# Value products in quarters over four steps, and positional tiles moved in halves of even and odd partitions

## The chip, the cores and the metric

The kernel runs on one core of one Trainium2 chip. The metric is the device time of one execution in microseconds; for the kernel before it is 3494.53 us, the median of 3 runs (3494.47 to 3496.61).

## What is computed

A Macaron layer over `x` of shape (8, 1024, 256), all in float32: half a feed-forward step, attention with relative positions, half a feed-forward step. What matters here is the attention (16 heads of 16 features, S = 1024):

```python
q = (xn @ Wq + bq).reshape(B, S, H, dh)      # k and v likewise
p = (pe @ Wp).reshape(S, H, dh)
content = jnp.einsum('bihd,bjhd->bhij', q + u_bias, k)
pos = jnp.einsum('bihd,jhd->bhij', q + v_bias, p)
pos = _relative_shift(pos)
attn = jax.nn.softmax((content + pos) * scale, axis=-1)
head = jnp.einsum('bhij,bjhd->bihd', attn, v).reshape(B, S, Dm)

def _relative_shift(pos_score):
    B, Hh, S1, S2 = pos_score.shape
    padded = jnp.concatenate([jnp.zeros((B, Hh, S1, 1), pos_score.dtype), pos_score], axis=-1)
    padded = padded.reshape(B, Hh, S2 + 1, S1)
    return padded[:, :, 1:].reshape(B, Hh, S1, S2)
```

The relative shift is a change of row pitch: rows written 1025 elements apart and read back 1024 apart come out shifted.

## The kernel before, in words

The program has three phases, one after the other: a front phase (first feed-forward step, layer norm, projections), the attention phase, and a closing phase (output projection, second feed-forward step). The change is in the attention phase alone.

The attention phase works on 128 units (batch times head) of 8 tiles each, so 1024 tiles. A tile is 128 query rows by 1024 keys, 512 KB in float32. Each engine runs the same numbered steps, 16 to a pass of its loop (`BODY = 16`, `rounds()`, L612 to L621); the first pass and the last, which is longer to drain what is under way, are written out, and the passes between are a hardware loop. In step `t`

- TensorE (`step`, L755) makes the content scores of tile `t` (`strips` into `ps_con`, L705) and the positional scores of tile `t + LEAD`, `LEAD = 8` (`strips` into `ps_pos`, L705). Both use 32 rows of the array each and run side by side. Then, in two steps of four, come the value products of the last complete group of four tiles (`times_values`, 32 matmuls in each of its two halves, L741), in another step one transpose that turns the heads back (`turn_heads`, L752), and in every step eight transposes of the finished scores of tile `t - 2` (`turn`, L729).
- ScalarE copies the positional scores of tile `t + 8` from PSUM to `pos_out`, a ring of 8 (`copy_positional`, L786), and takes the exponentials of tile `t - 2` (L795).
- SyncE, named SP in the profile, issues every DMA of the phase. It waits until `pos_out` of tile `t + 8` is copied and writes it to DRAM with pitch 1025 (`write`, L651); it then reads back, with pitch 1024, tile `t + 4` into `pos_in`, also a ring of 8 (`read_back`, L663), for which the write of tile `t + 5` must have landed. Steps 0, 1 and 2 of each unit also load queries (L633), keys (L640) and values (L646) of the next unit, and step 7 stores the heads of the last one (L669).
- VectorE adds content and positional scores and takes the row minimum of their negative (`total`, L818); before that it needs the read-back of tile `t` to have landed. In one step of four it copies the value products (L826), in the next it normalises the heads (L832, L837).
- GpSimd subtracts the maximum (L855).

There is one `ps_con`, so TensorE can start the content scores of tile `t + 1` only when VectorE has read those of tile `t` (`content_room`, L709). DRAM row `u` of block `g` of a tile (four blocks of 32 rows) lies in partition `4u + g`. `at_once` (L43) is a wait in an instruction of its own; on SP it blocks everything behind it, and so does each DMA while SP issues it.

Of the kernel before, what the change touches and what calls it, by code (L numbers as in the profile page):

```python
# [9 lines left out]
P = 128  # L10
B, S, D, H = 8, 1024, 256, 16
# [8 lines left out]
GAPS = 4  # L20
HALF = S // 2

TILES = S // P
UNITS = H * B
NT = UNITS * TILES
BODY = 2 * TILES
LEAD = 8
READ_LAG = 4
RING = 8
PITCH = S + 1  # L30
QUAD = 4
# [11 lines left out]
def at_once(eng, sem, value):  # L43

    eng.wait_ge(sem, value)
    eng.nop(nofuse=True)
# [491 lines left out]
def attention_phase(nc, keep, a):  # L538


    with ExitStack() as ctx:
        def sb(name, shape, dt=F32):
            return ctx.enter_context(nc.sbuf_tensor("at_" + name, shape, dt))
# [9 lines left out]

        pos_out = sb("pos_out", [P, RING, S])
        pos_in = sb("pos_in", [P, RING, S])
        neg_max = sb("neg_max", [P, RING])
        prob = [sb(f"prob{k}", [P, TILES, QUAD * P]) for k in range(2)]
# [9 lines left out]

        written, read = sems("written", RING), sems("read", RING)
        q_in, k_in, vals_in, head_out = (sems(n, 2) for n in ("q_in", "k_in", "vals_in", "head_out"))
# [6 lines left out]
        class Tile:  # L576
# [11 lines left out]

            def rounds(self, n, add=0):

                return self.r * (16 * BODY // n) + 16 * (self.t // n + add)

            def units(self, each=1, add=0):
                return self.r * (2 * each) + (self.unit_in_body * each + add)
# [17 lines left out]
        def rounds(eng, step):  # L612

            last = NT // BODY - 1
            for t in range(BODY):
                step(0, t)
            with eng.Fori(1, last) as r:
                for t in range(BODY):
                    step(r, t)
            for t in range(BODY + 10):  # L620
                step(last, t)  # L621

        score_dram = a["scores"]
# [2 lines left out]
        @block.sync  # L626
        def _(sp):
            def load_queries(u):
                if u.past(BODY):
                    at_once(sp, con_mm, u.units(TILES, -TILES))  # L630
                at_once(sp, pos_mm, u.units(TILES))
                rows = 2 * STRIP if u.last_unit() else P
                sp.dma_start(left[u.side][0:rows:2, :],  # L633
                             a["queries"][u.unit() + 1].rearrange("s d m -> (s d) m")[0:rows // 2, :])\
                    .then_inc(q_in[u.side], 16)

            def load_keys(u):
                if u.past(BODY):
                    at_once(sp, con_mm, u.units(TILES, -TILES))
                sp.dma_start(right[u.side][0:2 * STRIP:2, :], a["keys"][u.unit()].rearrange("n d m -> (n d) m"))\  # L640
                    .then_inc(k_in[u.side], 16)

            def load_values(u):
                if u.past(BODY):
                    at_once(sp, v_ready, u.units(1, -1))
                sp.dma_start(v_in[u.side][:, :], a["values"][u.unit(), :, :]).then_inc(vals_in[u.side], 16)  # L646

            def write(w):
                at_once(sp, pos_copied, w.count(1, 1))
                dst = score_dram[w.side, w.i * P * PITCH:(w.i + 1) * P * PITCH]  # L650
                sp.dma_start(dst.rearrange("(g u c) -> u g c", g=GAPS, c=PITCH)[:, :, 1:], pos_out[:, w.slot, :])\  # L651
                    .then_inc(written[w.slot], 16)

            def read_back(t):
                if t.i == 0:
                    at_once(sp, written[t.slot], t.rounds(RING, 1))
                if t.i + 1 < TILES:
                    n = Tile(t.r, t.t + 1)
                    at_once(sp, written[n.slot], n.rounds(RING, 1))
                if t.past(RING):  # L660
                    at_once(sp, turned, t.count(2, 2 - 2 * RING))
                src = score_dram[t.side, (t.i * P + 1) * S:(t.i * P + 1 + P) * S]
                sp.dma_start(pos_in[:, t.slot, :], src.rearrange("(g u c) -> u g c", g=GAPS, c=S))\  # L663
                    .then_inc(read[t.slot], 16)

            def store_head(t):

                at_once(sp, normed, t.units(2, 2))
                sp.dma_start(a["heads"][t.unit(), :, :].rearrange("(g u) n -> u g n", g=GAPS), head[t.side][:, :])\  # L669
                    .then_inc(head_out[t.side], 16)  # L670

            def step(r, t):
                w = Tile(r, t + LEAD)
                if w.real():
                    write(w)
                back = Tile(r, t + LEAD - READ_LAG)
                if back.real():
                    read_back(back)
                for at, load in ((0, load_queries), (1, load_keys), (2, load_values)):
                    if t % TILES == at and Tile(r, t - at + TILES).real():  # L680
                        load(Tile(r, t - at + TILES))
                done = Tile(r, t - TILES)
                if t % TILES == 7 and done.real():
                    store_head(done)

            sp.wait_ge(blanked, 1)
            sp.dma_start(left[1][2 * STRIP:P:2, :], a["queries"][0].rearrange("s d m -> (s d) m")[STRIP:2 * STRIP, :])\
                .then_inc(first_in, 16)
            load_queries(Tile(0, 0))
            load_keys(Tile(0, 0))  # L690
            load_values(Tile(0, 0))
            for w in range(LEAD):
                write(Tile(0, w))
                if w >= READ_LAG:
                    read_back(Tile(0, w - READ_LAG))
            rounds(sp, step)
            for k in range(2):
                sp.wait_ge(head_out[k], 16 * UNITS // 2)

        @block.tensor  # L700
        def _(pe):
# [28 lines left out]
                                           pos_in[:, t.slot, kt * P:(kt + 1) * P], keep["ident"][:, :])  # L730
                    ins.then_inc(turned, 1)

            def times_values(t, half):
                if half == 0:
                    pe.wait_ge(v_ready, t.units(1, 1))
                    pe.wait_ge(exped, t.count(2, 2 * QUAD))
                    if t.past(QUAD):
                        pe.wait_ge(pv_copied, t.quads())
                for kt in range(TILES // 2 * half, TILES // 2 * (half + 1)):
                    for g in range(QUAD):  # L740
                        ins = pe.matmul(ps_pv[VW * g:VW * (g + 1), :], v_aug[t.side][:, kt, :],  # L741
                                        prob[t.t // QUAD % 2][:, kt, g * P:(g + 1) * P],
                                        start=(kt == 0), stop=(kt == TILES - 1))
                if half == 1:
                    ins.then_inc(pv_mm, 1)

            def turn_heads(t):

                pe.wait_ge(pv_copied, t.quads(1))
                if t.past(QUAD):  # L750
                    pe.wait_ge(normed, t.quads())
                pe.transpose(ps_head[:, :, :].rearrange("p g v -> p (g v)"), head_T[:, :], keep["ident"][:, :])\  # L752
                    .then_inc(head_mm, 1)

            def step(r, t):  # L755
                if Tile(r, t).real():
                    content_room(Tile(r, t))
                if Tile(r, t + LEAD).real():
                    positional_room(Tile(r, t + LEAD))
                if Tile(r, t).real():  # L760
                    strips(Tile(r, t), Tile(r, t).side, 0, ps_con, con_mm)
                if Tile(r, t + LEAD).real():
                    strips(Tile(r, t + LEAD), Tile(r, t).side, 2 * STRIP, ps_pos, pos_mm)
                if t % QUAD == 2 and Tile(r, t - 6).real():
                    times_values(Tile(r, t - 6), 0)
                if t % QUAD == 3 and Tile(r, t - 7).real():
                    times_values(Tile(r, t - 7), 1)
                if t % QUAD == 1 and Tile(r, t - 9).real():
                    turn_heads(Tile(r, t - 9))
                if Tile(r, t - 2).real():  # L770
                    turn(Tile(r, t - 2))

# [37 lines left out]
        def _(dve):  # L810
# [11 lines left out]
            def copy_products(t):  # L822
                dve.wait_ge(pv_mm, t.quads(1))
                if t.past(QUAD):
                    dve.wait_ge(head_mm, t.quads())
                dve.tensor_copy(head_T[:, :], ps_pv[:, :]).then_inc(pv_copied, 1)  # L826
# [12 lines left out]
                                  ALU.mult).then_inc(normed, 1)  # L839

            def step(r, t):
                if Tile(r, t).real():
                    total(Tile(r, t))
                if t % QUAD == 0 and Tile(r, t - 8).real():
                    copy_products(Tile(r, t - 8))
                if t % QUAD == 1 and Tile(r, t - 9).real():
                    normalise(Tile(r, t - 9))

            rounds(dve, step)

# [284 lines left out]
```

## Time and profile before

| | |
|---|---|
| time, median of 3 runs | 3494.53 us |
| the profiled execution, its own time | 3496.67 us |
| its span | 3494.9 us |
| TensorE busy, share of the span | 3161.2 us, 90% |
| VectorE / ScalarE / GpSimd busy | 1711.3 / 2285.4 / 1330.7 us |
| DMA queue q1, share of 16 engines' span | 95.8% |
| attention, from the first to the last L818 | 337.3 to 3320.0 us |

The page gives each engine's busy time, then the span in 40 slices of 87 us: the attention phase fills slices 4 to 37. Issue instructions of DMAs are not counted as busy on SP; they are found in the timeline (as SPq) and by their source line.

### The profile page before, as it was taken

Reading aid. Unit: us, or ns where it says so; the run is one execution under the profiler, and the core shown is the slowest. Engines: PE = TensorE matmul, PEld = TensorE weight load, DVE = VectorE, ACT = ScalarE, POOL = GpSimd, SP = SyncE. Lnnn points to the kernel's source line nnn. Section 1 sums busy time; section 2 is a strip of 40 time slices with the busy share of each in tenths; the row PEclk is TensorE's granted clock in tenths of the full one; section 3 lists DMA queues with packets and bytes.
Section 4 is the critical chain, followed back from the end, with each engine's and each line's share of the span. In section 5 each row is a group of like instructions: output and inputs, shape, how many; then the busy total and the mean of one; then the engine's idle time right before and its main releaser. Section 6 shows DMA issues by size and latency. Waiting matters only on the chain. (4 is left out here: it accounts for less than half of the span.)

```text
span 3494.9 us, 104304 instructions
## 1 busy us (share of the span) xinstructions
PE 3161.2 (90%) x34876; PEld 1962.1 (56%) x34876; DVE 1711.3 (49%) x3603; ACT 2285.4 (65%) x3255; POOL 1330.7 (38%) x1341
## 2 busy tenths in 40 slices
PE   8996999999999999999999999999999999999988
PEld 5662555555555555555555555555555555555577
DVE  7771444444444444444444444444444444444457
ACT  3443777777767776777777777777777777777633
POOL 2111444444444444444444444444444444444410
PEclk9996999999999999999999999999999999999999
DMA  5977999999999999999999999999999999999862
GB/s 162 296 248 246 376 380 377 379 382 380 378 376 383 379 378 379 383 380 377 378 382 377 380 377 383 381 379 378 381 379 377 379 382 378 380 375 384 332 193 98
DMA packets 433552, 1231.26 MB, mean 352 GB/s; under 512 B 48992, under 2 KB 133472, under 8 KB 433504
## 3 DMA queue, kind: packets, MB, share of 16 engines
q1 hardware_dynamic: 430000, 1229.12, 95.8%
q10 hardware_dynamic: 3504, 1.53, 0.2%
q8 instruction: 27, 0.44, 0.1%
q14 instruction: 21, 0.17, 0.0%
HBM read 617.04 MB, written 613.43 MB: 352 GB/s over the span
## 5 line engine op out<-in xcount | busy, mean ns | idle before, releaser
L818 DVE CUSTOM_DVE_ANT_0 at_pos_in<-at_ps_con,at_pos_in 128x1024 f32<-128x1024 f32 x1024 | 1254.2, 1225 | 1621.7 <-PE at_ps_con L705 1184.4
L855 POOL TENSOR_SCALAR at_pos_in<-at_pos_in,at_neg_max 128x1024 f32<-128x1024 f32 x1024 | 1149.4, 1122 | 1720.3 <-DVE at_neg_max L818 1720.3
L786 ACT ACTIVATE at_pos_out<-at_ps_pos 128x1024 f32<-128x1024 f32 x1024 | 1050.0, 1025 | 651.7 <-PE at_ps_pos L705 651.7
L705 PE MATMUL at_ps_con<-at_right,at_left 32*128 32x512 f32 x4096 | 1157.3, 641 | 262.7 <-DVE at_neg_max L818 261.4
L795 ACT ACTIVATE at_prob<-at_ps_turn 128x512 f32<-128x512 f32 x2048 | 1109.1, 596 | 277.5 <-PE at_ps_turn L729 277.4
L705 PE MATMUL at_ps_pos<-at_right,at_left 32*128 32x512 f32 x4096 | 1164.9, 645 | 28.5 <-DMA at_left<-scratch_queries 20.6
L729 PE MATMUL at_ps_turn<-keep_ident,at_pos_in 128*128 128x128 f32 x8192 | 1105.3, 278 | 0.6 <-ACT at_prob L795 0.6
L729 PEld LDWEIGHTS at_ps_turn<-keep_ident,at_pos_in 128*128 128x128 f32 x8192 | 889.7, 141 | 299.0 <-ACT at_prob L795 188.1
L741 PEld LDWEIGHTS at_ps_pv<-at_prob,at_v_aug 128*32 128x32 f32 x16384 | 416.1, 109 | 387.8 <-issue 246.7
L705 PEld LDWEIGHTS at_ps_con<-at_right,at_left 32*128 32x128 f32 x4096 | 309.5, 183 | 471.7 <-ACT at_pos_out L786 367.6
L741 PE MATMUL at_ps_pv<-at_prob,at_v_aug 128*32 128x128 f32 x16384 | 553.2, 276 | 0.8 <-issue 0.8
L705 PEld LDWEIGHTS at_ps_pos<-at_right,at_left 32*128 32x128 f32 x4096 | 308.6, 184 | 39.9 <-POOL at_v_aug L893 21.0
L752 PEld LDWEIGHTS at_ps_head<-keep_ident,at_head_T 128*128 128x128 f32 x256 | 35.3, 138 | 193.3 <-issue 192.7
L872 POOL COPY at_right<-keep_pos_keys 64x512 f32 (+1 forms) x128 | 78.0, 610 | 37.3 <-POOL at_pos_in L855 20.4
L818 DVE DVE_READ_ACCUMULATOR2_ANT at_neg_max<- 128x1 f32 x1024 | 85.1, 83 | 0.0
L752 PE MATMUL at_ps_head<-keep_ident,at_head_T 128*128 128x128 f32 x256 | 83.8, 328 | 0.4 <-DVE at_head_T L826 0.4
L382 ACT ACTIVATE fr_qk<-fr_ps_qk,keep_b_qk 128x512 f32<-128x512 f32 x64 | 64.4, 1177 | 24.9 <-PE fr_ps_qk L332 24.9
L826 DVE COPY at_head_T<-at_ps_pv 128x128 f32<-128x128 f32 x256 | 73.4, 287 | 3.6 <-PE at_ps_pv L741 3.6
L534 POOL TENSOR_TENSOR fr_scale<-fr_variance,keep_minus_half 128x4 f32<-128x4 f32 x16 | 30.6, 1912 | 116.1 <-DVE fr_variance L456 116.1
L374 ACT ACTIVATE fr_z1T<-fr_ps_a 128x1024 f32<-128x1024 f32 x16 | 16.4, 1026 | 84.1 <-PE fr_ps_a L80 84.1
L1069 POOL TENSOR_TENSOR cl_scale<-cl_variance,keep_minus_half 128x4 f32<-128x4 f32 x16 | 16.1, 1009 | 134.9 <-DVE cl_variance L1051 134.9
L837 DVE TENSOR_TENSOR at_head<-at_ps_head,at_inverse 128x64 f32<-128x64 f32 x256 | 57.6, 225 | 14.3
(90 smaller groups left out, 1296.2 us busy)
## 6 DMA issues: line engine op xcount, KB each, us to landing
scratch_scores<-at_pos_out SPq DMA_DIRECT2D x1024, 512.0 KB, 6.5
at_pos_in<-scratch_scores SPq DMA_DIRECT2D x1024, 512.0 KB, 6.8
scratch_queries<-fr_qk SPq DMA_DIRECT2D x128, 256.0 KB, 4.0
at_left<-scratch_queries SPq DMA_DIRECT2D x127, 256.0 KB, 6.3
fr_x<-in_L_attn_x_dram SPq DMA_DIRECT2D x16, 512.0 KB, 6.0
scratch_x<-fr_x_bo SPq DMA_DIRECT2D x16, 512.0 KB, 5.0
scratch_keys<-fr_qk SPq DMA_DIRECT2D x32, 256.0 KB, 5.0
scratch_values<-fr_values SPq DMA_DIRECT2D x8, 1024.0 KB, 5.8
```

The source lines that it names most:

```text
L382: ins = act.activation(qk[k][:, o, f, :].rearrange("p (t u g) -> p t g u", u=P // GAPS, g=GAPS), ps_qk[:, f, :].rearrange("p (t g u) -> p ...
L705: ins = pe.matmul(banks[:, n, :], left[side][rows, t.i * P:(t.i + 1) * P], right[side][rows, :], start=True, stop=True)
L729: ins = pe.transpose(ps_turn[:, n, j * P:(j + 1) * P], pos_in[:, t.slot, kt * P:(kt + 1) * P], keep["ident"][:, :])
L741: ins = pe.matmul(ps_pv[VW * g:VW * (g + 1), :], v_aug[t.side][:, kt, :], prob[t.t // QUAD % 2][:, kt, g * P:(g + 1) * P], start=(kt == 0) ...
L752: pe.transpose(ps_head[:, :, :].rearrange("p g v -> p (g v)"), head_T[:, :], keep["ident"][:, :])\
L786: act.activation(pos_out[:, t.slot, :], ps_pos[:, :, :].rearrange("p a m -> p (a m)"), ACT.Copy)\
L795: act.activation(prob[t.t // QUAD % 2][:, 4 * n:4 * n + 4, k * P:(k + 1) * P], ps_turn[:, n, :].rearrange("p (j i) -> p j i", i=P), ACT.Exp)\
L818: dve.tensor_tensor_reduce(pos_in[:, t.slot, :], ps_con[:, :, :].rearrange("p a m -> p (a m)"), pos_in[:, t.slot, :], -SCALE, 3.0e38, ALU. ...
L826: dve.tensor_copy(head_T[:, :], ps_pv[:, :]).then_inc(pv_copied, 1)
L837: dve.tensor_tensor(head[t.side][:, :].rearrange("p (t d) -> p t d", d=DH)[:, QUAD * q:QUAD * (q + 1), :], ps_head[:, :, 0:DH], inverse[:, ...
L855: pool.tensor_scalar(pos_in[:, t.slot, :], pos_in[:, t.slot, :], -1.0, neg_max[:, t.slot:t.slot + 1], ALU.mult, ALU.add).then_inc(shifted, 1)
L872: pool.tensor_copy(right[1 - u.side][P // 2:P, :], keep["pos_keys"][P // 2:P, bass.ds(u.unit() % H * HALF, HALF)]).then_inc(p_ready, 1)
```

## The change

The value products of a group of four tiles, so far 32 matmuls in each of two steps, come as 16 in each of four steps; the transpose of the heads, the copy and the normalisation on VectorE move one or two steps later, and on VectorE they stand ahead of the step's `total` instead of behind it. The last pass has 12 further steps instead of 10.

Every positional tile is written as two DMAs of 64 partitions (even ones, then odd ones) and read back the same way. SP's step now reads: wait for the copy, wait for the landed write, write the even half of tile `t + 8`, read the even half of tile `t + 4`, write the odd half, read the odd half. Each DMA is 256 KB. The wait for `turned` ahead of a read is kept only where no write precedes it. A ring slot's semaphore now counts 32 a tile.

```diff
@@ BODY, counts @@
+PARTS = 2
...
-                return self.r * (16 * BODY // n) + 16 * (self.t // n + add)
+                return self.r * (16 * PARTS * BODY // n) + 16 * PARTS * (self.t // n + add)
...
-            for t in range(BODY + 10):
+            for t in range(BODY + 12):
@@ SyncE @@
-            def write(w):
+            def part(rows, n):
+                return rows[:, n:GAPS:PARTS]
+
+            def may_write(w):
                 at_once(sp, pos_copied, w.count(1, 1))
+
+            def write(w, n):
                 dst = score_dram[w.side, w.i * P * PITCH:(w.i + 1) * P * PITCH]
-                sp.dma_start(dst.rearrange("(g u c) -> u g c", g=GAPS, c=PITCH)[:, :, 1:], pos_out[:, w.slot, :])\
+                sp.dma_start(part(dst.rearrange("(g u c) -> u g c", g=GAPS, c=PITCH)[:, :, 1:], n),
+                             pos_out[n:P:PARTS, w.slot, :])\
                     .then_inc(written[w.slot], 16)
...
-                if t.past(RING):
-                    at_once(sp, turned, t.count(2, 2 - 2 * RING))
+
+            def read_back(t, n):
                 src = score_dram[t.side, (t.i * P + 1) * S:(t.i * P + 1 + P) * S]
-                sp.dma_start(pos_in[:, t.slot, :], src.rearrange("(g u c) -> u g c", g=GAPS, c=S))\
+                sp.dma_start(pos_in[n:P:PARTS, t.slot, :],
+                             part(src.rearrange("(g u c) -> u g c", g=GAPS, c=S), n))\
                     .then_inc(read[t.slot], 16)
+
+            def write_and_read(w, back):
+                if w.real():
+                    may_write(w)
+                elif back.real():
+                    at_once(sp, turned, back.count(2, 2 - 2 * RING))
+                if back.real():
+                    may_read(back)
+                for n in range(PARTS):
+                    if w.real():
+                        write(w, n)
+                    if back.real():
+                        read_back(back, n)
@@ TensorE @@
-                if t % QUAD == 2 and Tile(r, t - 6).real():
-                    times_values(Tile(r, t - 6), 0)
-                if t % QUAD == 3 and Tile(r, t - 7).real():
-                    times_values(Tile(r, t - 7), 1)
-                if t % QUAD == 1 and Tile(r, t - 9).real():
-                    turn_heads(Tile(r, t - 9))
+                part = (t - 6) % QUAD
+                if Tile(r, t - 6 - part).real():
+                    times_values(Tile(r, t - 6 - part), part)
+                if part == 0 and Tile(r, t - 10).real():
+                    turn_heads(Tile(r, t - 10))
@@ VectorE @@
+                if t % QUAD == 2 and Tile(r, t - 10).real():
+                    copy_products(Tile(r, t - 10))
+                if t % QUAD == 3 and Tile(r, t - 11).real():
+                    normalise(Tile(r, t - 11))
                 if Tile(r, t).real():
                     total(Tile(r, t))
-                if t % QUAD == 0 and Tile(r, t - 8).real():
-                    copy_products(Tile(r, t - 8))
-                if t % QUAD == 1 and Tile(r, t - 9).real():
-                    normalise(Tile(r, t - 9))
```

On SP, in the loop, the step that also loads the next unit's values and the step behind it stood like this before (names are DRAM and SBUF tensors, the numbers are the DMA's shape):

```order
L651 DMA scratch_scores<-at_pos_out 32x4x1024 [waits at_pos_copied]
L45 REGISTER_ALU [waits at_written7]
L663 DMA at_pos_in<-scratch_scores 128x1x1024 [waits at_turned]
L646 DMA at_v_in<-scratch_values 128x128 [waits at_v_ready]
L45 REGISTER_ALU
L651 DMA scratch_scores<-at_pos_out 32x4x1024 [waits at_pos_copied]
L663 DMA at_pos_in<-scratch_scores 128x1x1024 [waits at_turned]
```

and stand like this now:

```order
L657 DMA scratch_scores<-at_pos_out 32x2x1024 [waits at_pos_copied,at_written7]
L670 DMA at_pos_in<-scratch_scores 64x1x1024
L657 DMA scratch_scores<-at_pos_out 32x2x1024
L670 DMA at_pos_in<-scratch_scores 64x1x1024
L647 DMA at_v_in<-scratch_values 128x128 [waits at_v_ready]
L46 REGISTER_ALU
L657 DMA scratch_scores<-at_pos_out 32x2x1024 [waits at_pos_copied]
L670 DMA at_pos_in<-scratch_scores 64x1x1024
L657 DMA scratch_scores<-at_pos_out 32x2x1024
L670 DMA at_pos_in<-scratch_scores 64x1x1024
```

Two issues a step have become four, back to back; the wait for `turned` is gone, and the wait for the landed write now stands ahead of the write of the same step.

On TensorE, one step of the loop with value products, before:

```order
L705 MATMUL at_ps_pos<-at_right,at_left 128x512 x2
L741 MATMUL at_ps_pv<-at_prob,at_v_aug 32x128 x16
L726 REGISTER_ALU [waits at_shifted]
L729 MATMUL at_ps_turn<-keep_ident,at_pos_in 128x128 [waits at_exped]
L729 MATMUL at_ps_turn<-keep_ident,at_pos_in 128x128 x3
```

and now:

```order
L719 MATMUL at_ps_pos<-at_right,at_left 128x512 x2
L756 MATMUL at_ps_pv<-at_prob,at_v_aug 32x128 x8
L740 REGISTER_ALU [waits at_shifted]
L743 MATMUL at_ps_turn<-keep_ident,at_pos_in 128x128 [waits at_exped]
L743 MATMUL at_ps_turn<-keep_ident,at_pos_in 128x128 x3
```

The row of value products (16 instructions here, 32 matmuls in the trace) is half as long and stands in each of four steps instead of two.

## Rows read from the trace of the kernel before

**Rows 1.** The page, the span in 40 slices: TensorE, its clock, DMA share, rate.
```profile
PE   8996999999999999999999999999999999999988
...
PEclk9996999999999999999999999999999999999999
DMA  5977999999999999999999999999999999999862
GB/s 162 296 248 246 376 380 377 379 382 380 378 376 383 379 378 379 383 380 377 378 382 377 380 377 383 381 379 378 381 379 377 379 382 378 380 375 384 332 193 98
```

**Rows 2.** Windows: an early stretch of 10 us and a steady one of 1000 us.
```profile
core 0: us, PE busy (x) PEld busy (x) DVE busy (x) ACT busy (x) POOL busy (x), PEclk, DMA share, GB/s
370.00:380.00 10.00, 9.23 (x121) 5.87 (x113) 5.45 (x11) 7.25 (x11) 3.81 (x5) 1.00 1.03 403
1000.00:2000.00 1000.00, 912.55 (x11059) 549.89 (x11054) 468.05 (x945) 705.51 (x1030) 421.03 (x429) 1.00 1.02 379
```

**Rows 3.** Source line L818: duration in ns, first and last start.
```profile
L818 DVE CUSTOM_DVE_ANT_0 at_pos_in<-at_ps_con,at_pos_in x1024: 1224/1225/1226, 337.3 to 3320.0; 128x1024 f32<-128x1024 f32 x171
```

**Rows 4.** Timeline, steady stretch: start, length, engine, line, what; idle before.
```profile
1511.75 0.70 PE L705 MATMUL at_ps_con<-at_right,at_left 32*128 32x512 f32 x2
...
1512.82 1.08 PE L741 MATMUL at_ps_pv<-at_prob,at_v_aug 128*32 128x128 f32 x32
...
1513.83 1.09 PE L729 MATMUL at_ps_turn<-keep_ident,at_pos_in 128*128 128x128 f32 x8
...
1514.86 0.70 PE L705 MATMUL at_ps_con<-at_right,at_left 32*128 32x512 f32 x2
...
1515.93 1.09 PE L729 MATMUL at_ps_turn<-keep_ident,at_pos_in 128*128 128x128 f32 x8
...
1516.23 1.23 DVE L818 CUSTOM_DVE_ANT_0 at_pos_in<-at_ps_con,at_pos_in 128x1024 f32<-128x1024 f32 x1 [1.87 <-PE at_ps_con L705]
...
1517.38 0.08 DVE L818 DVE_READ_ACCUMULATOR2_ANT at_neg_max<- 128x1 f32 x1
...
1517.59 0.70 PE L705 MATMUL at_ps_con<-at_right,at_left 32*128 32x512 f32 x2 [0.57 <-DVE at_neg_max L818]
```

**Rows 5.** Waits of the SP queue in 1000 to 2000 us: total, times, longest.
```profile
SPq L46 <- ACT at_pos_out L786: 303.2, 304, 1.8
```

**Rows 6.** Timeline of the SP queue, steady stretch.
```profile
1508.25 0.57 SPq L651 DMA_DIRECT2D scratch_scores<-at_pos_out  x1
1509.04 0.53 SPq L663 DMA_DIRECT2D at_pos_in<-scratch_scores  x1
1509.82 1.02 SPq L640 DMA_DIRECT2D at_right<-scratch_keys  x1
...
1514.09 0.55 SPq L651 DMA_DIRECT2D scratch_scores<-at_pos_out  x1
1514.74 0.54 SPq L663 DMA_DIRECT2D at_pos_in<-scratch_scores  x1
```

**Rows 7.** Source lines of SP: issue time in ns (min/median/max), first and last start.
```profile
L651 SPq DMA_DIRECT2D scratch_scores<-at_pos_out x1024: 517/552/854, 312.6 to 3298.2; - x171
...
L663 SPq DMA_DIRECT2D at_pos_in<-scratch_scores x1024: 513/529/1393, 326.0 to 3304.9; - x171
...
L633 SPq DMA_DIRECT2D at_left<-scratch_queries x128: 539/547/841, 307.5 to 3279.5; - x128
...
L640 SPq DMA_DIRECT2D at_right<-scratch_keys x128: 589/998/1293, 308.1 to 3282.1; - x128
...
L646 SPq DMA_DIRECT2D at_v_in<-scratch_values x128: 490/940/1397, 308.7 to 3284.6; - x128
...
L669 SPq DMA_DIRECT2D scratch_heads<-at_head x128: 588/595/1101, 383.8 to 3328.7; - x128
```

**Rows 8.** Timeline of the SP queue ahead of the attention's first tile.
```profile
307.51 0.54 SPq L633 DMA_DIRECT2D at_left<-scratch_queries  x1
308.10 0.59 SPq L640 DMA_DIRECT2D at_right<-scratch_keys  x1
308.74 0.58 SPq L646 DMA_DIRECT2D at_v_in<-scratch_values  x1
```

**Rows 9.** Source line L951 of the closing phase: issue time in ns.
```profile
L951 SPq DMA_DIRECT2D out_dram<-cl_out x16: 372/372/378, 3374.1 to 3491.5; - x16
```

**Rows 10.** Timeline of the SP queue in the front phase: eight stores in a row.
```profile
102.34 5.59 SPq L216 DMA_DIRECT2D scratch_queries<-fr_qk  x8
```

**Rows 11.** The page, DMA issues: KB each, median us to landing.
```profile
at_pos_in<-scratch_scores SPq DMA_DIRECT2D x1024, 512.0 KB, 6.8
```

More of the change, by code:

```diff
@@ L646, in load_values, with may_read @@
                 sp.dma_start(v_in[u.side][:, :], a["values"][u.unit(), :, :]).then_inc(vals_in[u.side], 16)
-            def write(w):
+            def part(rows, n):
+                return rows[:, n:GAPS:PARTS]
+            def may_write(w):
                 at_once(sp, pos_copied, w.count(1, 1))
+            def write(w, n):
                 dst = score_dram[w.side, w.i * P * PITCH:(w.i + 1) * P * PITCH]
-                sp.dma_start(dst.rearrange("(g u c) -> u g c", g=GAPS, c=PITCH)[:, :, 1:], pos_out[:, w.slot, :])\
+                sp.dma_start(part(dst.rearrange("(g u c) -> u g c", g=GAPS, c=PITCH)[:, :, 1:], n),
+                             pos_out[n:P:PARTS, w.slot, :])\
                     .then_inc(written[w.slot], 16)
-            def read_back(t):
+            def may_read(t):
                 if t.i == 0:
@@ L672, in step @@
             def step(r, t):
[L673 to L678, printed above, removed]
+                write_and_read(Tile(r, t + LEAD), Tile(r, t + LEAD - READ_LAG))
                 for at, load in ((0, load_queries), (1, load_keys), (2, load_values)):
@@ L692, in _ @@
             for w in range(LEAD):
-                write(Tile(0, w))
-                if w >= READ_LAG:
-                    read_back(Tile(0, w - READ_LAG))
+                write_and_read(Tile(0, w), Tile(0, w - READ_LAG))
             rounds(sp, step)
@@ L731, in turn, with times_values @@
                     ins.then_inc(turned, 1)
-            def times_values(t, half):
-                if half == 0:
+            def times_values(t, part):
+                if part == 0:
                     pe.wait_ge(v_ready, t.units(1, 1))
@@ L738, in times_values @@
                         pe.wait_ge(pv_copied, t.quads())
-                for kt in range(TILES // 2 * half, TILES // 2 * (half + 1)):
+                for kt in range(TILES // QUAD * part, TILES // QUAD * (part + 1)):
                     for g in range(QUAD):
@@ L743, in times_values @@
                                         start=(kt == 0), stop=(kt == TILES - 1))
-                if half == 1:
+                if part == QUAD - 1:
                     ins.then_inc(pv_mm, 1)
```

## The prediction

> **What bounds the kernel now.** I read the 40 slices first [rows 1]: the attention phase fills slices 4 to 37 of 40, and there TensorE, its clock and the DMA engines all stand at 9, so everything is decided in one steady loop. The windows give that loop in numbers [rows 2]: over 1000 us TensorE is busy for 912.55 us at a granted clock of 1.00, that is the 2.4 GHz level, and the DMA engines show a share of 1.02 at 379 GB/s. Two resources look full, so the question is which one the step waits for. Line L818 runs once a tile; from its first to its last start are 3320.0 - 337.3 = 2982.7 us, and over 1023 steps that is 2.916 us a step [rows 3].
>
> The timeline tells what a step is made of [rows 4]. A step with value products goes from 1511.75 to 1514.86, 3.11 us, and TensorE never idles: 1.07 us of scores (to 1512.82), 1.01 us of products (to 1513.83), 1.03 us of transposes. A step without them goes from 1514.86 to 1517.59, 2.73 us, and its last 0.57 us are idle: the content scores wait for VectorE, which starts L818 at 1516.23 and is through at 1517.46. So half of the steps are bound by TensorE's own work (3.11) and half by the chain content scores, VectorE, content scores (2.73); their mean, 2.92, is the step measured. Neither names a DMA: the engines stand full, yet what they bring is in time.
>
> The third queue is SP, which issues all DMAs. Its waits show 303.2 us of idling in 1000 us, all for the positional copy [rows 5]. A thousand us are 343 steps, so SP idles 0.88 us a step and works for 2.916 - 0.88 = 2.03 us (the view's 1000 - 303.2, by 343 steps). It is not the bound, but 0.88 us is all it has to give.
>
> **TensorE's part.** The same 64 product matmuls a group are dealt as 16 to a step. Each step then has 1.07 + 0.51 + 1.03 = 2.61 us of TensorE work [rows 4], below the chain's 2.73, and in the step with the head transpose about 0.2 more, 2.8. Every step would be near 2.73: per group of four tiles 2 x (3.11 - 2.73) = 0.76 us, 0.19 us a step, 194 us over 1023 steps. The copy and the normalisation on VectorE move ahead of `total`; they lie in its idle 1.87 us before L818 [rows 4], so I cost them at nothing, and if that cover were gone they would add at most their own busy time, under 0.2 us a step (the 468.05 us of VectorE in 1000 us less L818's 1.225 and its 0.08 leave 0.06 us a step). Two more steps of draining at the end hold only a quarter of the products each; I take 1 to 2 us. This gain exists only if nothing else sets the step.
>
> **SP's part.** Now the cost. Per step SP issues four DMAs of 64 partitions instead of two of 128. The issue of a full write takes 0.552 us, of a full read 0.529 [rows 7]. What is an issue of half the rows worth? The trace has a DMA of just that size: the load of queries, 64 rows of 4 KB into every second partition, at 0.547 [rows 7]. The key load, with a quarter of its bytes and half of its partitions, took 0.59 when nothing stood ahead, the value load, 128 short rows, 0.58 [rows 8]. So the issue does not shrink with the rows, and I take 0.545. The gaps: two issues with no wait between stand 0.05 us apart (307.51 + 0.54 to 308.10) [rows 8]; write and read stood 0.22 apart with two waits between (1508.82 to 1509.04) and 0.10 with one (1514.64 to 1514.74) [rows 6], so a wait that is already met costs 0.11. Before: 0.22 of gaps. After: 0.11 for the wait for the landed write and 3 x 0.05, together 0.26, so 0.04 more, although the wait for `turned` goes.
>
> One thing gets cheaper. Keys and values take 0.998 and 0.940 us to issue in the loop [rows 7] but 0.59 and 0.58 on an idle queue [rows 8]: there SP is held by the backlog of full tiles ahead of it. If SP is what limits, the backlog goes, and 0.77 us in eight steps, 0.10 a step, come back. I take this, and keep its absence for the range.
>
> Per step: 2.03 - (0.552 + 0.529) + 4 x 0.545 + 0.04 - 0.10 = 3.07 us of SP's own work. That is more than 2.916, the step now, and more than the 2.73 that the engines would do. SP is in order and has no idle left, so **its 3.07 us become the step**: 0.154 x 1023 = 158 us, with the drain 160. What is late next is the read-back: it is issued four steps ahead and takes 6.8 us to land [rows 11], so SP falls behind until `total` waits for it on VectorE; TensorE waits for VectorE and ScalarE for TensorE. The positional copy, for which SP waits today, is then always ready.
>
> By this the profiled execution becomes 3496.67 + 160 = 3656.7 us. The median of the runs shown lies 2.1 us below the profiled one, so the forecast is **3655 us**, +4.6%. The bounds of the issue: 0.513, the shortest full read [rows 7], gives 2.94 a step and 3522; 0.595, the head store [rows 7], gives 3.27 and 3860. With 0.545 and the held-up keys and values kept the step is 3.17 and the time 3757. The break-even with the kernel before lies at an issue of 0.506 us ((2.916 - 0.89) / 4), below each of the 1024 reads and 1024 writes.
>
> On what an issue costs a rule speaks the other way. The Trainium skill, page "DMA: Bandwidth & Descriptors", section "Issuing engines are not separate DMA queues", holds that the sequencer's time to initiate a DMA is usually small relative to the DMA itself. By it SP's term would be nought and the time about 3303 us. The trace does not agree: two issues are 1.08 us of a step of 2.916.
>
> **The rivals.**
>
> *The issue is short, and the engines' gain shows (faster).* The closing phase issues its output, 512 KB from all partitions, in 0.372 us [rows 9], so an issue can be short. If the halved shapes fell into that kind, SP's step were 0.89 + 4 x 0.372 = 2.38 and out of the way. It decides below 0.506 us. Then the step goes to 2.73, or to what the DMA engines do: 379 GB/s x 2.916 / 2.73 = 405 GB/s, where the best 10 us show 403 [rows 2], so 2.74. That is 180 us less, 3315 us. Against it: the output's shape is met nowhere in this loop, and all six sorts of issue in it, whatever their size, have medians of 0.529 us or more [rows 7].
>
> *SP is not the bound, and the DMA engines are (no change, or a little faster).* Their share is 1.02 over 1000 us of the loop [rows 2]. If 379 GB/s is what they can do with this mix, TensorE's gain turns into a wait of `total` for the read-back, and the step stays between 2.87 and 2.916: 3450 to 3495 us. It needs an issue below 0.506 too. For it: the full share; against it: 403 GB/s once [rows 2], and no wait for a DMA today. The halves are meant to mix reads and writes more finely in each engine's queue, which could raise the rate; no row shows that it does. The Trainium skill, same page, section "Rules for kernel authors", says of two transfers to disjoint halves of the partitions: "Don't bother — they serialize". By it the halves win nothing in the DMA engines, and with SP out of the way this rival would be the outcome, at about 3494 us. No run here shows two such halves yet.
>
> *Four issues in a row hold one another up (much slower).* Eight stores of 256 KB in a row took 5.59 us in the front phase, 0.70 each [rows 10]. At 0.65 an issue, SP's step is 3.49 and the time 4083. Against it: there the queue was fed at 256 KB in 0.70 us, here 1 MB comes in three us, and the three loads in a row took 0.54 to 0.59 [rows 8].
>
> *The change does not do what it says.* The order of instructions shows both parts, four issues a step and half the products a step, so I leave it no chance of its own.
>
> **How the numbers follow.** SP as the bound with an issue between 0.51 and 0.58: 0.71, likeliest 3655. Held up further: 0.07. Short issue and engines' gain: 0.13. DMA-bound without SP: 0.09, about half of it within 0.2% (7 us, about what a measurement of this kernel can tell from no change). So slower 0.77 (nearly all of the first two cases), same 0.05, faster 0.18. The range leaves out the 0.07 above and the 0.13 below: from 3470, inside the DMA-bound case, to 3810, an issue of 0.58 with the backlog gone. The forecast's own range, without the cases of other sign, is 3505 to 3810.
>
> **What would show it.** In the profile after: SP's waits for the positional copy near nought in place of 303.2 us; the half issues with medians between 0.53 and 0.58 us, 4096 of them in all, each right behind the other; L818's successor with a wait for the DMA of `at_pos_in` and 3.0 to 3.1 us a step; TensorE's idle time larger although each step's own work is 2.61 us and even from step to step; a DMA rate down to some 360 GB/s; keys and values issued in about 0.6 us. The TensorE clock stays at 1.00 in my sum, since no slice of the loop shows it lower [rows 1]. I am wrong if the half issue comes out under 0.51 us, or if SP still idles for the copy while the step is shorter than 2.916.

## The result and the profile after

The changed kernel takes **3754.16 us** (median of 4 runs, 3753.50 to 3756.42), the kernel before on the same chip 3495.57 us (3494.47 to 3497.12): ratio 1.0741, with a 95% interval of [1.0722, 1.0759]. It is 259 us slower; 160 were forecast. The profiled execution took 3754.51 us, its span is 3752.7 us, and 3655 stood in the forecast.

The page of the changed kernel, the span in 40 slices, answers to [rows 1]:

```profile
PE   8996888888888888888888888888888888888888
...
PEclk9997999999999999999999999999999999999999
DMA  5987999999999999999999999999999999999953
GB/s 174 283 262 264 335 347 349 351 348 348 350 349 348 348 352 347 350 349 347 349 350 351 346 352 350 346 351 350 347 348 351 348 347 349 353 346 350 350 178 111
```

TensorE falls from 9 to 8 tenths in every slice of the attention, its clock stays, and the DMA engines move about 350 GB/s in place of about 380. Their busy digit is still 9. The window of 1000 us, busy us and instructions of TensorE, its weight loads, VectorE, ScalarE and GpSimd, then clock, DMA share and GB/s, against [rows 2]:

```profile
1000.00:2000.00 1000.00, 873.48 (x10195) 500.88 (x10194) 430.19 (x869) 667.22 (x949) 387.01 (x395) 0.99 0.98 349
```

Every engine does less in the same time, and the clock has not moved (0.99 for 1.00, both the 2.4 GHz level), so the step is longer. L832 is the old L818. Its source line (ns min/median/max, first and last start) gives (3576.9 - 337.0) / 1023 = 3.167 us a step, where [rows 3] gave 2.916:

```profile
L832 DVE CUSTOM_DVE_ANT_0 at_pos_in<-at_ps_con,at_pos_in x1024: 1224/1225/1227, 337.0 to 3576.9; 128x1024 f32<-128x1024 f32 x171
```

What does it wait for? The waits of 1000 to 2000 us (total, times, longest) have a line that the kernel before did not have:

```profile
DVE at_pos_in L832 <- DMA at_pos_in<-scratch_scores: 407.7, 202, 3.7
```

The read-back is late. The same view for the SP queue, which held one line of 303.2 us [rows 5], is empty now: SP waits for nothing in a thousand microseconds. That is the signature of a queue that is itself the bound. The source lines of SP's issues, in ns, against [rows 7]:

```profile
L657 SPq DMA_DIRECT2D scratch_scores<-at_pos_out x2048: 517/590/1152, 312.2 to 3558.8; - x187
...
L670 SPq DMA_DIRECT2D at_pos_in<-scratch_scores x2048: 513/597/2529, 325.7 to 3567.3; - x187
...
L634 SPq DMA_DIRECT2D at_left<-scratch_queries x128: 525/542/609, 307.0 to 3539.5; - x128
...
L641 SPq DMA_DIRECT2D at_right<-scratch_keys x128: 517/521/1125, 307.6 to 3542.8; - x128
...
L647 SPq DMA_DIRECT2D at_v_in<-scratch_values x128: 471/481/872, 308.2 to 3546.0; - x128
```

By the medians a half write costs 0.590 us and a half read 0.597, where a whole one cost 0.552 and 0.529: half the bytes, and no less time on SP. Keys and values came down from 0.998 and 0.940 to 0.521 and 0.481. The timeline of SP (start, length) shows where the extra 0.05 us sits, and what a step of SP is:

```profile
1501.72 0.55 SPq L657 DMA_DIRECT2D scratch_scores<-at_pos_out  x1
1502.32 0.61 SPq L670 DMA_DIRECT2D at_pos_in<-scratch_scores  x1
1502.98 0.60 SPq L657 DMA_DIRECT2D scratch_scores<-at_pos_out  x1
1503.62 0.61 SPq L670 DMA_DIRECT2D at_pos_in<-scratch_scores  x1
1504.46 0.55 SPq L657 DMA_DIRECT2D scratch_scores<-at_pos_out  x1
...
1507.27 0.59 SPq L690 DMA_DIRECT2D scratch_heads<-at_head  x1
1508.56 0.56 SPq L657 DMA_DIRECT2D scratch_scores<-at_pos_out  x1
...
1511.44 0.55 SPq L634 DMA_DIRECT2D at_left<-scratch_queries  x1
1512.21 0.56 SPq L657 DMA_DIRECT2D scratch_scores<-at_pos_out  x1
...
1514.98 0.52 SPq L641 DMA_DIRECT2D at_right<-scratch_keys  x1
1515.72 0.55 SPq L657 DMA_DIRECT2D scratch_scores<-at_pos_out  x1
...
1518.35 0.49 SPq L647 DMA_DIRECT2D at_v_in<-scratch_values  x1
1519.02 0.55 SPq L657 DMA_DIRECT2D scratch_scores<-at_pos_out  x1
...
1530.02 0.55 SPq L657 DMA_DIRECT2D scratch_scores<-at_pos_out  x1
...
1532.86 0.59 SPq L690 DMA_DIRECT2D scratch_heads<-at_head  x1
1533.68 0.56 SPq L657 DMA_DIRECT2D scratch_scores<-at_pos_out  x1
```

The first of four takes 0.55 us, the three right behind it 0.59 to 0.63 from 1501 to 1530. A step with nothing else takes 2.74 us (1501.72 to 1504.46), much the same as the 2.73 of the chain of content scores and VectorE [rows 4]. The four steps that also load or store take 4.10 (head store, and the loop's branch behind it), 3.65, 3.51 and 3.30 us. Four plain steps at 2.74 and these four make 25.5 us for eight, 3.19 a step. The branch comes only with every second head store; the next one's step takes 3.66 (1530.02 to 1533.68), and with the mean of the two it is 3.16 a step, where 3.167 was measured: SP's own work is the step.

TensorE's timeline in the same place (idle time before, with its releaser, in brackets):

```profile
1502.94 1.09 PE L743 MATMUL at_ps_turn<-keep_ident,at_pos_in 128*128 128x128 f32 x8
1504.87 0.70 PE L719 MATMUL at_ps_con<-at_right,at_left 32*128 32x512 f32 x2 [0.84 <-DVE at_neg_max L832]
...
1505.94 0.65 PE L756 MATMUL at_ps_pv<-at_prob,at_v_aug 128*32 128x128 f32 x16
1506.52 1.09 PE L743 MATMUL at_ps_turn<-keep_ident,at_pos_in 128*128 128x128 f32 x8
1507.60 0.70 PE L719 MATMUL at_ps_con<-at_right,at_left 32*128 32x512 f32 x2
```

From 1504.87 to 1507.60 is 2.73 us, with products in it: the even step that the change was to bring is there, and it is as short as forecast. Then TensorE waits for VectorE, which waits for SP's read-back, and the mean is 3.167.

### The profile page after: what moved, and what is told of

Read it like the earlier page. It is cut to its first block and busy times, and to the rows that moved or that the text cites. A ratio compares the mean times of both kernels' runs of the same rounds, so it can differ in the third digit from the quotient of the medians.

```text
span 3752.7 us, 104410 instructions
## 1 busy us (share of the span) xinstructions
PE 3271.3 (87%) x34876; PEld 1947.0 (52%) x34876; DVE 1711.4 (46%) x3603; ACT 2339.8 (62%) x3255; POOL 1326.6 (35%) x1341
## 5 line engine op out<-in xcount | busy, mean ns | idle before, releaser
L832 DVE CUSTOM_DVE_ANT_0 at_pos_in<-at_ps_con,at_pos_in 128x1024 f32<-128x1024 f32 x1024 | 1254.2, 1225 | 1879.3 <-DMA at_pos_in<-scratch_scores 1276.3
L756 PEld LDWEIGHTS at_ps_pv<-at_prob,at_v_aug 128*32 128x32 f32 x16384 | 387.9, 110 | 780.1 <-issue 770.8
L756 PE MATMUL at_ps_pv<-at_prob,at_v_aug 128*32 128x128 f32 x16384 | 664.9, 281 | 0.8 <-issue 0.8
L832 DVE DVE_READ_ACCUMULATOR2_ANT at_neg_max<- 128x1 f32 x1024 | 85.0, 83 | 0.0
```

The lines of the kernel that those rows point to most:

```text
L832: dve.tensor_tensor_reduce(pos_in[:, t.slot, :], ps_con[:, :, :].rearrange("p a m -> p (a m)"), pos_in[:, t.slot, :], -SCALE, 3.0e38, ALU. ...
```

## The experiments

Ratios are against the kernel before on the same chip, whose median lay between 3495 and 3497 us each time.

### Which part costs: the products alone, the halves alone

**e1_quarters**, the kernel before with TensorE's and VectorE's part alone; its DMAs stay whole:

```diff
-                if t % QUAD == 2 and Tile(r, t - 6).real():
-                    times_values(Tile(r, t - 6), 0)
-                if t % QUAD == 3 and Tile(r, t - 7).real():
-                    times_values(Tile(r, t - 7), 1)
+                part = (t - 6) % QUAD
+                if Tile(r, t - 6 - part).real():
+                    times_values(Tile(r, t - 6 - part), part)
```

> Products in quarters alone, DMAs whole as before. Theory A (the loss is all SP's issue time, and SP has 0.88 us a step to spare here): nothing takes TensorE's gain, the step goes from 2.916 to 2.73 to 2.80 us, 3310 to 3380 us. Rival B (the DMA engines are full at 379 GB/s and hold the step): 3450 to 3495 us, with waits of L818's successor for the read-back. Rival C (the products' place costs, for instance in VectorE's order): over 3495 us.

The diff shows TensorE's part; VectorE's is as in the change. Measured: 3514.62 us, 1.0047 [1.0030, 1.0064]. The gain did not come; the kernel is even a little slower. Its window and its waits in 1000 to 2000 us, first SP's, then VectorE's:

```profile
1000.00:2000.00 1000.00, 934.51 (x10957) 535.20 (x10957) 462.16 (x933) 716.49 (x1020) 416.19 (x425) 1.00 1.02 376
```

```profile
SPq L46 <- ACT at_pos_out L786: 231.2, 254, 2.1
SPq L46 <- DMA scratch_scores<-at_pos_out: 83.5, 161, 1.7
...
DVE at_pos_in L818 <- DMA at_pos_in<-scratch_scores: 338.2, 207, 2.6
```

SP idles 315 us, so it isn't SP's own work. A read-back now lands 9.5 us after its issue (6.8 before [rows 11]), and VectorE waits for it: TensorE's gain runs into the DMAs. These are the signs of rival B, 20 us above its range. The time alone would fit rival C, but e4 and e7 below have the products in the same places and are faster than the kernel before. Whether the rate of the DMA engines or the fixed lead of four steps (`READ_LAG`) makes the read-back late was not told apart: no run changes the lead.

**e2_halves**, the changed kernel with the old products: the halves alone.

```diff
-                for kt in range(TILES // QUAD * part, TILES // QUAD * (part + 1)):
+                for kt in range(TILES // 2 * half, TILES // 2 * (half + 1)):
```

> DMAs in halves alone, products in two steps as before. Theory A: SP's work is the step, whatever TensorE does: 3754 us within 10, SP without a wait for the positional copy. Rival C (part of the loss is the new places of the products): 3500 to 3700 us.

Measured: 3755.63 us, 1.0749 [1.0731, 1.0767], a step of 3.167 us and no wait of SP in the view. The whole loss is in the halves, and with them in place the products' order is worth nothing.

### Is it the number of issues on SP?

**e3_write_halves**: old products, the write in halves, the read whole, so three issues a step, in the changed kernel's order of waits.

```diff
+W_PARTS, R_PARTS = 2, 1
...
+                for n in range(2):
+                    if w.real() and n < W_PARTS:
+                        write(w, n)
+                    if back.real() and n < R_PARTS:
+                        read_back(back, n)
```

> Products as before; only the writes in halves, reads whole: three issues a step. Theory A: SP's work is 2.03 - 1.08 + 0.55 + 0.59 + 0.60 = 2.69 us a step, below 2.916: no change, 3495 us within 7, SP still idle some 0.2 us a step. Rival D (smaller DMAs are themselves slower to move, half of them cost half of the loss): about 3620 us.

Measured: 3495.59 us, 0.9998 [0.9988, 1.0007]. SP's waits:

```profile
SPq L47 <- ACT at_pos_out L800: 132.8, 194, 1.1
SPq L47 <- DMA scratch_scores<-at_pos_out: 2.2, 8, 0.9
```

At 343 steps SP idles 0.39 us a step, from 0.88 before: the third issue is paid out of idle time and costs nothing. The fourth no longer fits.

**e9_halves_old_products_act**: the halves alone as in e2, but the loads of queries, keys and values and the head store are issued by ScalarE; SP keeps the four halves.

```diff
@@ SyncE @@
-                for at, load in ((0, load_queries), (1, load_keys), (2, load_values)):
-                    if t % TILES == at and Tile(r, t - at + TILES).real():
-                        load(Tile(r, t - at + TILES))
@@ ScalarE @@
+                for at, load in ((0, load_queries), (1, load_keys), (2, load_values)):
+                    if t % TILES == at and Tile(r, t - at + TILES).real():
+                        load(act, Tile(r, t - at + TILES))
```

> Halves, products in two steps as before, loads and head store on ScalarE. Theory A: SP's work is 2.79 us, below the 2.916 of the engines: the time of the kernel before, 3495 us within 15; the 258 us go though every half DMA is still there. Rival E (the halves cost by themselves): over 3600 us.

Measured: 3497.54 us, 1.0003 [0.9994, 1.0013]. All the halves are there, with all their bytes and packets, and the 7.5% are gone. SP waits 45.1 us of 1000 again, which makes its work 954.9 / 343 = 2.78 us a step. Against e2 only the four small DMAs have moved, out of SP and so out of its queue.

**e12_two_of_four_on_act** is the dose between: the changed kernel with queries and keys alone moved to ScalarE.

```diff
+                for at, load in ((0, load_queries), (1, load_keys)):
```

> The changed kernel with the loads of queries and keys alone on ScalarE; values and head store stay on SP. Theory A as a dose: in the profile after, the queries cost SP 0.92 us and the keys 0.76 us a unit beyond an ordinary gap, 1.68 / 8 = 0.21 us a step; SP's work and so the step fall from 3.17 to 2.96 us and the time to 3540 us within 15. A rival in which the DMA engines or the products set a part of the step would leave it above 3600 us.

Measured: 3534.77 us, 1.0109 [1.0092, 1.0126], SP without a wait. In the changed kernel's timeline those two steps were 3.65 and 3.51 us where a plain one is 2.74; without them (0.91 + 0.77) / 8 = 0.21 us a step goes, 215 us of the run, and 219 went: at this dose the kernel's time follows SP's. VectorE's line gives a step of 2.953 us:

```profile
L834 DVE CUSTOM_DVE_ANT_0 at_pos_in<-at_ps_con,at_pos_in x1024: 1224/1225/1226, 336.8 to 3358.1; 128x1024 f32<-128x1024 f32 x171
```

### What TensorE's gain is worth with SP out of the way

**e4_write_halves_quarters**: the changed kernel, reads whole again (three issues).

```diff
-PARTS = 2
+W_PARTS, R_PARTS = 2, 1
```

> The changed kernel with reads whole: three issues a step and products in quarters. Theory A: SP's work 2.69 us, by itself just below the 2.73 of content scores and VectorE: within 30 us of the kernel with quarters alone. Rival B: 3450 to 3495 us. Rival D: about 3620 us.

Measured: 3466.41 us, 0.9911 [0.9894, 0.9927]. Faster than before, at 381 GB/s, with VectorE waiting 251.4 us in 1000 for the read-back. That is rival B's range; it lies 48 us under e1, outside theory A's 30.

**e7_whole_new_order** separates the halves from the changed order of SP's waits in e4: both DMAs whole, the changed kernel's order.

```diff
-PARTS = 2
+W_PARTS, R_PARTS = 1, 1
```

> Products in quarters, writes and reads whole, but in the changed kernel's order: the wait for the landed write ahead of the write, no wait for turned. Theory B: 3515 us within 10, as with quarters alone, since the engines see the same DMAs. Rival F (the gain of write halves came from the order of waits): 3466 us.

Measured: 3485.34 us, 0.9966 [0.9952, 0.9980], neither e1's time nor e4's, so both expectations missed. The order of the waits (landed write ahead of the write, none for `turned`) brings 29 us against e1 and the halved write 19 more. By which way the order helps was not found. Its source line of the read settles another point:

```profile
L670 SPq DMA_DIRECT2D at_pos_in<-scratch_scores x1024: 513/596/1467, 325.7 to 3298.7; - x171
```

A whole read right behind the write takes 0.596 us, where it took 0.529 with waits between [rows 7], and a half read 0.597. What costs more is the place in the row and not the half.

**e8_read_halves_quarters**: writes whole, reads in halves.

```diff
-PARTS = 2
+W_PARTS, R_PARTS = 1, 2
```

> Products in quarters, writes whole, reads in halves: three issues a step, SP 2.69 us. Theory G (any halving lets the slowest of the 16 DMA engines catch up): 3466 us within 15, as with write halves. Rival H (only write halves help): 3515 us within 10.

Measured: 3576.40 us, 1.0225 [1.0208, 1.0242]: both expectations missed, with three issues a step as in e4. SP waits for nothing. Its timeline, where x2 is the two reads together:

```profile
1500.55 0.57 SPq L657 DMA_DIRECT2D scratch_scores<-at_pos_out  x1
1501.17 1.57 SPq L670 DMA_DIRECT2D at_pos_in<-scratch_scores  x2
...
1504.31 1.64 SPq L670 DMA_DIRECT2D at_pos_in<-scratch_scores  x2
```

Two reads in a row hold SP for some 1.6 us here (up to 2.14 in the 25 us from 1500), where a read and a write in turn take 1.26 (1502.32 to 1503.58 above). By VectorE's line the step is (3402.5 - 337.8) / 1023 = 3.00 us, all of it SP's, where the count of three issues gave 2.69. The rival of issues that hold one another up is real in this order, and not in the order of the change.

**e5_halves_loads_on_act**: the whole change, with the four small DMAs on ScalarE as in e9.

> The changed kernel with the loads of queries, keys and values and the store of the heads issued by ScalarE; same DMAs, same waits. Theory A (SP's own work is the step): SP loses (0.54 + 0.52 + 0.48 + 0.59 and about 0.9 of waits and gaps) / 8 = 0.38 us a step, 3.17 becomes 2.79, and the time falls by at least 280 us, to 3370 to 3470 us, the upper end if the DMA engines hold the step. Rival E (DMAs of 256 KB in turn are what the DMA engines move slower, 349 GB/s being their rate for them): 3740 to 3760 us.

Measured: **3414.98 us, 0.9766 [0.9750, 0.9783]**, faster than both kernels. Its window, L832 and the waits:

```profile
1000.00:2000.00 1000.00, 968.54 (x11388) 556.63 (x11387) 481.27 (x971) 744.87 (x1059) 432.14 (x442) 1.00 1.02 390
```

```profile
L832 DVE CUSTOM_DVE_ANT_0 at_pos_in<-at_ps_con,at_pos_in x1024: 1223/1225/1227, 337.9 to 3238.5; 128x1024 f32<-128x1024 f32 x171
```

```profile
DVE at_pos_in L832 <- DMA at_pos_in<-scratch_scores: 202.9, 134, 2.1
...
SPq L47 <- DMA scratch_scores<-at_pos_out: 25.3, 71, 1.1
```

A step is 2.835 us and the rate 390 GB/s, the highest sustained in these runs. SP works 974.7 / (1000 / 2.835) = 2.76 us of it.

**e10_whole_loads_on_act**, e5's control: the same with whole DMAs.

```diff
-PARTS = 2
+W_PARTS, R_PARTS = 1, 1
```

> Products in quarters, whole DMAs in the changed kernel's order, loads and head store on ScalarE: the control for the 3415 us of halves with loads on ScalarE. Theory I (what makes that one fast is the halves, by which the DMA engines move more): about 3485 us, 375 to 382 GB/s, SP with time to spare. Rival J (moving the loads off SP does it): 3415 us within 15.

Measured: 3459.85 us, 0.9899 [0.9882, 0.9915], at 384 GB/s, between the two expectations. So moving the loads brings 25 us (e7 to e10), although SP idled 310 us of 1000 in e7 already; why was not found. The halves in turn bring 45 us (e10 to e5), once SP has room for them.

**e6_write_halves_loads_on_act**, e4 with the loads moved:

> The kernel with products in quarters and writes in halves, reads whole, and these loads on ScalarE. Theory B (there the DMA engines are the bound, not SP): within 10 us of 3466, or a little less. If SP with its 2.69 us still bounds it: about 3380 us.

Measured: 3451.47 us, 0.9876 [0.9860, 0.9893], 15 us under e4, at 385 GB/s. SP idles 245 us of 1000 for written tiles to land, and that buys next to nothing: its own work isn't the bound here. VectorE waits 259.8 us for the read-back.

**e11_two_writes_two_reads_act**: e5, but write, write, read, read.

```diff
                 for n in range(PARTS):
                     if w.real():
                         write(w, n)
+                for n in range(PARTS):
                     if back.real():
                         read_back(back, n)
```

> Halves, products in quarters, loads on ScalarE, but both write halves first and then both read halves, no longer in turn. Theory K (the second of two halves in the same direction is held up as it is issued, as with reads in halves after a whole write, where two took 1.6 us): SP's work rises by 0.4 to 0.8 us a step, 3700 to 4200 us. Rival L (the turn does not matter): 3415 us within 15.

Measured: 3516.28 us, 1.0066 [1.0049, 1.0083], 101 us slower than e5 by the order alone, where one theory expected none and the other far more. The timeline of its SP:

```profile
1498.53 1.20 SPq L663 DMA_DIRECT2D scratch_scores<-at_pos_out  x2
1499.78 1.37 SPq L676 DMA_DIRECT2D at_pos_in<-scratch_scores  x2
1501.31 1.20 SPq L663 DMA_DIRECT2D scratch_scores<-at_pos_out  x2
1502.56 1.31 SPq L676 DMA_DIRECT2D at_pos_in<-scratch_scores  x2
```

Two writes in a row cost no more than a read and a write in turn (1.26). Two reads take 1.24 to 1.48 us in the 40 us from 1490, and once 2.18; the 13 pairs average 1.42, which is 0.16 more. SP's waits fall from 25.3 to 6.6 us of 1000: it is full again. VectorE's line gives the step:

```profile
L833 DVE CUSTOM_DVE_ANT_0 at_pos_in<-at_ps_con,at_pos_in x1024: 1223/1224/1227, 338.3 to 3338.4; 128x1024 f32<-128x1024 f32 x171
```

It is 2.933 us, of which SP works 2.91, 0.15 more than in e5. Of these 0.05 come out of its idle time and 0.10 lengthen the step, which is the 101 us. So SP's queue accounts for them; what holds the second read of a pair there was not found.

## Why the prediction was right, and where its size was off

**Direction and mechanism held.** SP's work per step passes the step and becomes it. What was to be seen is there: SP's waits 0 for 303.2, 2 x 2048 half issues, VectorE waiting for the DMA of `at_pos_in`, TensorE idling, its even step of 2.73 us, 349 GB/s where some 360 stood, the clock unmoved. Beyond the profile, e9 takes the loss away by giving SP room and nothing else, and e12 does so by the right dose.

**TensorE's part held as far as it went.** Its 0.19 us a step was said to exist only if nothing else sets the step. e2 and the changed kernel, with old and new products, are 1.5 us apart: worth nothing here.

**The issue of a half was mis-sized.** The step "so I take 0.545" rested on the load of queries [rows 7], an issue with a gap ahead of it. The first half of each step did cost that, 0.55; the other three, right behind another DMA, cost 0.60. That price stood in [rows 8]: the loads of keys and values there, at 0.59 and 0.58, follow 0.05 us behind another issue. The text read them as issues with nothing ahead. The medians are 0.590 and 0.597, just above the text's limit of 0.58 for the forecast's own case. With 0.575 for the mean of the writes and 0.597 for the reads the sum has 2.34 instead of 2.18, 0.16 a step more.

**The keys and values held, a little larger.** (0.998 - 0.521 + 0.940 - 0.481) / 8 = 0.117 us a step came back, 0.10 was taken. The reason given, that the backlog goes if SP is what limits, is not borne out, so the size was in part luck. In e3 SP still idles and the rate is 379 GB/s as before, yet keys and values cost 0.540 and 0.475. The runs in which SP issues them behind a whole read (the kernel before, e1, e7) have 0.82 to 1.05, those with a half DMA just ahead 0.35 to 0.54. That a held-up load needs a whole read ahead of it is what these runs suggest; none tests it by itself.

**The sum with these sizes** is 2.03 - 1.08 + 2.34 + 0.04 - 0.12 = 3.21 us against 3.167 measured. The last 0.04 is not assigned; gaps ahead of waits that are met are what the sum knows least. In time: 3.07 gave 160 us, 3.167 gives 0.251 x 1023 = 257, and 259 were measured.

**The range** held it. Its upper end is not what its words give: an issue of 0.58 makes 3.21 us a step and some 3798 us, not 3810. 3757 was in the text as the time of a step of 3.17 us, but for another reason (keys and values held up still), so its nearness is chance.

**The rivals.** *The short issue* did not happen: no half issue took less than 0.513 us, and 0.506 was the break-even. The Trainium skill, page "DMA: Bandwidth & Descriptors", section "Issuing engines are not separate DMA queues", calls the time to initiate a DMA usually small relative to the DMA. One by one that is so here, 0.6 us against 4.7 to landing. But landings overlap and the issues of one queue do not: four of them are 2.35 us, three quarters of the step, and SP's term was far from nought.

*Four issues holding one another up* did not come in the change's order: 0.60 and not 0.65. In e8 and e11 two reads in a row were held up.

*The DMA engines as the bound without SP* is, by its signs, the outcome with products in quarters as soon as SP has room: VectorE waits for the read-back in e1, e4, e6, e7 and e10, though the lead of four steps could have a part in it. I put it at 3450 to 3495 us; e4, e6, e7 and e10 lie there, e1 20 us above, e5 35 below. No run had TensorE's 194 us; the best one, e5, is 82 us faster than the kernel before, and part of that is the halves.

*The rule on halves.* e5 against e10 is 45 us, 1.3%, for halves in turn against whole tiles; in pairs, as in e11, they lose 56 us against e10. The Trainium skill, page "DMA: Bandwidth & Descriptors", section "Rules for kernel authors", says of disjoint halves not to bother, as they serialize. With SP full, or with the halves in pairs, that is good advice here; in turn and with SP free, e5 doesn't bear it out. A pair of halves of one transfer was not timed by itself, so whether they serialize is open: what e5 has over e11 is reads and writes in turn.

**What stays open.** Whether SP (2.76 of 2.835 us) or the DMA engines hold e5; whether a read-back issued more than four steps ahead would give TensorE's gain more room; why e7's order of waits beats e1's by 29 us; why reads in a row are held up and writes are not.

## What to carry to other kernels

Before splitting a DMA, count the issues of the in-order queue that sends it: here the issues of 256 and 512 KB in this loop cost 0.53 to 0.60 us alike, so two more a step needed 1.2 us where the queue idled 0.88. If the split is wanted, make room first by giving small loads to an engine with idle time; the same halves went from +7.4% to -2.3%. And when one engine's work is evened out, look at what is full beside it: in e1 VectorE's new waits for the read-back, 338.2 us of 1000, took the place of the whole gain of 194 us.

## What was not expected of the hardware

- **An issue right behind another costs about 0.05 us more**: 0.55 for the first half write of a step, 0.59 to 0.63 for the second. A whole read took 0.529 with waits ahead and 0.596 right behind a write (e7).
- **Reads in a row are held up**: behind a whole write, two half reads took 1.57 and 1.64 us (e8), behind two half writes 1.24 to 1.48 and once 2.18 (e11), in turn with writes about 0.6 each.
- **The DMA share doesn't tell how much is left**: 0.98 at 349 GB/s, 1.02 at 376 and at 390, 1.03 at 369 in e8, with the same bytes a tile. The rate and the waits told more.
- **The same load costs different times to issue, and the issuing engine isn't the reason**: the load of values took 0.481 us of SP's queue in the changed kernel, 0.353 of ScalarE's in e5, but 0.347 of SP's in e12. The lines of e5 and e12; the cause is open:

```profile
L642 ACTq DMA_DIRECT2D at_v_in<-scratch_values x127: 344/353/390, 346.7 to 3202.7; - x127
```

```profile
L642 SPq DMA_DIRECT2D at_v_in<-scratch_values x128: 343/347/1298, 308.1 to 3326.8; - x128
```

- **Order alone**: the same four halves on the same queues took 3415 us in turn and 3516 in pairs.
